# Second expert layer of a four-layer network: gate and up weights held still in one product, odd blocks stored from ScalarE's queue

## The reference

```python
logits = flat @ router_w.T
topk_scores, topk_idx = jax.lax.top_k(logits + router_bias, TOPK)      # TOPK = 2
topk_scores = jax.nn.softmax(topk_scores, axis=-1)
...
up_all = jnp.einsum('nd,kde->nke', flat, up_proj)       # (16, 128, 64)
gate_all = jnp.einsum('nd,kde->nke', flat, gate_proj)   # (16, 128, 64)
hidden = jax.nn.silu(gate_all) * up_all
down_all = jnp.einsum('nke,ked->nkd', hidden, down_proj)  # (16, 64, 128)
out = jnp.einsum('nk,nkd->nd', combine, down_all)
out = out + (jax.nn.silu(flat @ sh_gate.T) * (flat @ sh_up.T)) @ sh_down.T
```

## Time and profile before

| | us |
|---|---|
| Median of 3 runs | 928.29 |
| Lowest and highest run | 923.62, 928.73 |
| Span of the profiled execution, first to last instruction | 909.0 |
| The second layer's blocks, from the first gate-and-up product to the end of the last result copy | 484.60 to 536.16 |
| First TensorE instruction of the next attention | 538.38 |

### The profile page before, as it was taken

One profiled execution on the slowest core, in us unless ns is written; L12 is line 12 of the kernel. 1 busy time (PEld: TensorE's weight loads), 2 busy tenths in 40 slices (PEclk: granted clock), 3 DMA queues, 4 the chain that ended last, 5 costly groups with the idle time before them and its releaser, 6 DMA issues. The chain is left out here.

```text
span 909.0 us, 21425 instructions
## 1 busy us (share of the span) xinstructions
PE 777.9 (86%) x6462; PEld 591.8 (65%) x6462; DVE 599.4 (66%) x1816; ACT 504.2 (55%) x1391; POOL 414.8 (46%) x720
## 2 busy tenths in 40 slices
PE   3999996898679999999979977999969768669991
PEld 1566664798456778777747763666659546449991
DVE  5899995344567889888655447799947727633333
ACT  1577774676256776677635633677754422226663
POOL 3247766000534556765450018466217806824541
PEclk9999997999799999999989986799989775569996
DMA  8999941432000000100004431000000331122214
GB/s 254 384 401 404 289 195 35 90 90 57 23 7 14 14 15 24 26 22 11 19 25 100 114 85 28 16 23 23 2 1 2 98 102 41 46 54 64 74 51 153
DMA packets 69278, 78.96 MB, mean 87 GB/s; under 512 B 12848, under 2 KB 58560, under 8 KB 68912
## 3 DMA queue, kind: packets, MB, share of 16 engines
q1 hardware_dynamic: 59072, 62.15, 21.4%
q0 software_dynamic: 6368, 13.38, 5.1%
q10 hardware_dynamic: 3728, 2.07, 0.9%
HBM read 31.61 MB, written 45.96 MB: 85 GB/s over the span
## 5 line engine op out<-in xcount | busy, mean ns | idle before, releaser
L330 POOL DMA_INDIRECT routed_region<-routed_lines,line_slots x96 | 96.5, 1005 | 27.5 <-issue 23.6
L362 POOL DMA_INDIRECT late_results<-routed_region,line_slots x64 | 63.4, 990 | 77.4 <-remote 61.3
L774 ACT ACTIVATE probs_keymajor<-banks 128x512 f32<-128x512 f32 x128 | 70.2, 595 | 40.4 <-PE banks L584 40.4
L1401 PE MATMUL banks<-exps,work 128*128 128x128 f32 x624 | 85.5, 282 | 5.2 <-ACT exps L1475 5.0
L265 POOL TENSOR_TENSOR small<-small,half_and_eps 128x1 f32<-128x1 f32 x144 | 82.0, 569 | 11.3
L550 PE MATMUL banks<-work 32*128 32x512 f32 x256 | 80.9, 711 | 4.2 <-DVE exps L667 3.2
L658 DVE TENSOR_REDUCE small<-banks 128x8 f32<-128x1024 f32 x64 | 77.6, 1212 | 7.9 <-PE banks L550 3.9
L1401 PEld LDWEIGHTS banks<-exps,work 128*128 128x128 f32 x624 | 77.8, 196 | 7.5 <-ACT exps L1475 7.3
L667 DVE TENSOR_TENSOR exps<-banks,small 128x1024 f32<-128x1024 f32 x64 | 77.7, 1214 | 0.3
L584 PE MATMUL banks<-consts,exps 128*128 128x128 f32 x512 | 74.7, 294 | 1.1 <-ACT work L805 1.1
L584 PEld LDWEIGHTS banks<-consts,exps 128*128 128x128 f32 x512 | 61.1, 152 | 19.2 <-issue 13.0
(11 more groups left out here) (277 smaller groups left out, 1888.3 us busy)
## 6 DMA issues: line engine op xcount, KB each, us to landing
routed_region<-mid SPq DMA_DIRECT2D x52, 528.0 KB, 5.5
exps<-routed_region SPq DMA_DIRECT2D x125, 66.0 KB, 1.9
routed_region<-work SPq DMA_DIRECT2D x86, 64.0 KB, 1.8
weights_f<-in_weights_f SPq DMA_DIRECT2D x1, 4096.0 KB, 18.0
weights_f<-in_weights_f SPq DMA_DIRECT2D x3, 1024.0 KB, 10.9
shifted_rows<-work SPq DMA_DIRECT2D x16, 128.0 KB, 1.7
work<-expert_results SPq DMA_DIRECT2D x8, 256.0 KB, 5.0
routed_region<-routed_lines,line_slots POOLq DMA_INDIRECT x96, 2.4
```

Of the source, the lines that this page charges most:

```text
L330: nc.gpsimd.indirect_dma_start(k.regions[layer % 2], bass.IndirectOffsetOnAxis(k.slots[:, b, j:j + 1], 0), k.line[:, b % LINES, j, :], Non ...
L362: nc.gpsimd.indirect_dma_start(k.late[:, b % 2, j, :], None, k.regions[layer], bass.IndirectOffsetOnAxis(k.slots[:, b, j:j + 1], 0)).then_ ...
L774: nc.scalar.activation(k.pT[:, g * 512:(g + 1) * 512], bank[:, PT + g % 2, :], ACT.Copy).then_inc(s.pT, 1)
L1401: last = nc.tensor.matmul(bank[:, 2 + m % 4, i * T:(i + 1) * T], tile.weights[:, m % COPIES, i * 128:(i + 1) * 128], tile.gotT[:, m % 2, : ...
```

## The change

In the second layer the weights now take the way of the first layer, with GpSimd as the copier:

- GpSimd, after it has cleared the semaphores, copies each block's 128 columns of gate and up weights into the ring of four tiles (L1457 of the kernel before, now with `wide` = 128 columns).
- `up` waits for that copy, holds these weights still and streams the transposed tokens. Partitions 0 to 63 of the result are the up features, 64 to 127 the gate features (the two weight loads of the sublayer swap places), each 128 tokens long. The results use four banks of PSUM in place of two.
- ScalarE applies SiLU from partitions 64 to 127 into partitions 0 to 63, 128 elements each; VectorE multiplies into `tile.hid`, 64 partitions by 128, a ring of three. The lower half of `tile.hid` is zeroed once.
- The transpose of the inner values on TensorE and its copy on ScalarE are gone; `down` reads `tile.hid` directly.
- SyncE stores the even blocks only. ScalarE's queue stores the odd ones, four steps behind (`STORE_LAG`), inside ScalarE's loop; for that ScalarE reads the rows of the odd blocks into registers, four values at a time, every second entry of `rows_i`.

The diff, cut to its core:

```diff
-    t.hid = split(w[:, 0:2 * hidden], hidden)
+    t.hid = split(w[:, 0:3 * T], T)
...
-                for i, from_ in enumerate((E1 * H1, 0)):
+                for i, from_ in enumerate((0, E1 * H1)):
...
+    STORE_LAG = 4
+
+    def store(queue, m, row):
+        queue.wait_ge(s.y_out, m + 1)
+        queue.dma_start(region[bass.ds(row, T), 0:D], tile.y[:, m % RING, :]).then_inc(ld.stored[m % RING], 16)
...
-            if linear and m >= RING + 3:
-                store(m - RING - 3)
+            if linear and m >= RING + 3 and not (narrow and (m - RING - 3) % 2):
+                store(sp, m - RING - 3, rows_[m - RING - 3])
...
-            if m > 1:
-                pe.wait_ge(s.hid, m - 1)
-            nc.tensor.matmul(bank[:, 2 + m % 2, 0:wide], tile.gotT[:, m % 2, :], ups[:, bass.ds(offs[m], wide)],
-                             start=True, stop=True).then_inc(s.up, 1)
+            pe.wait_ge(s.copied, m + 1)
+            if m >= 4:
+                pe.wait_ge(s.hidT, m - 3)
+            for i in range(wide // T):
+                last = nc.tensor.matmul(bank[:, 2 + m % 4, i * T:(i + 1) * T],
+                                        tile.weights[:, m % COPIES, i * 128:(i + 1) * 128], tile.gotT[:, m % 2, :],
+                                        start=True, stop=True)
+            last.then_inc(s.up, 1)
...
-            if 0 <= t - 1 < nb and not by_feature:
-                hidden_T(t - 1)
...
-            copy(tile.weights[:, m % COPIES, :], ups[:, bass.ds(offs[m] * unit, 512)]).then_inc(s.copied, 1)
+            copy(tile.weights[:, m % COPIES, 0:wide], ups[:, bass.ds(offs[m] * unit, wide)]).then_inc(s.copied, 1)
...
+            if narrow:
+                nc.scalar.activation(tile.gate[0:H1, m % 2, 0:T], bank[H1:2 * H1, 2 + m % 4, 0:T],
+                                     ACT.Silu).then_inc(s.act, 1)
+                return
...
+        def store_odd(m):
+            if m // 2 == len(odd_rows):
+                odd_rows.extend(registers(mybir.EngineType.Activation, row_i[:, m:min(m + 8, nb):2],
+                                          REGIONS[layer % 2] * SHARE - T))
+            store(act, m, odd_rows[m // 2])
...
+        for t in range(-1, nb + (STORE_LAG if narrow else 2)):
...
-            if not by_feature and 0 <= t - 1 < nb:
-                hidden_T(t - 1)
+            if narrow and t >= STORE_LAG and (t - STORE_LAG) % 2:
+                store_odd(t - STORE_LAG)
...
+        if narrow:
+            v.memset(tile.hid[H1:128, :, :], 0.0).then_inc(s.padded, 1)
...
+            if narrow:
+                v.tensor_tensor(tile.hid[0:H1, m % hidden_ring, :], tile.gate[0:H1, m % 2, 0:T],
+                                bank[0:H1, 2 + m % 4, 0:T], ALU.mult).then_inc(s.hidT, 1)
                 return
...
+        if narrow:
+            copied = copy_weights(pool, mybir.EngineType.Pool, nc.gpsimd.tensor_copy, [], 1)
+            pool.wait_ge(s.steps, OFFS)
+            for m in range(nb):
+                copied(m)
```

More of the change, by code:

```diff
@@ L1223, in expert_layer @@
     biased = not gated
-    by_feature = hidden > H1
+    narrow = layer == 1
     tile = expert_tiles(k, max(hidden, 128), n, biased)
@@ L1230, in expert_layer @@
         s.act, = sems.new(tag, "act", True)
[L1231 to L1234, removed]
+    s.copied, = sems.new(tag, "copied", True)
     if shared:
@@ L1246, in expert_layer @@
     chunks = max(1, hidden // 128)
-    hidden_ring = 3 if by_feature else 2
+    hidden_ring = 3
     wide = 2 * hidden if gated else hidden
@@ L1395, in up, with down @@
             pe.wait_ge(s.xT_out, m + 1)
[L1396 to L1405, removed]
-            if m > 1:
-                pe.wait_ge(s.hid, m - 1)
-            nc.tensor.matmul(bank[:, 2 + m % 2, 0:wide], tile.gotT[:, m % 2, :], ups[:, bass.ds(offs[m], wide)],
-                             start=True, stop=True).then_inc(s.up, 1)
-        def hidden_T(m):
+            pe.wait_ge(s.copied, m + 1)
[6 more added lines that the diff above has]
+            last.then_inc(s.up, 1)
+        def down(m):
+            pe.wait_ge(s.hidT, m + 1)
             if shared and m == 0:
                 pe.wait_ge(s.sadd, 4)
[L1414 to L1423, removed]
+                pe.wait_ge(s.padded, 1)
             if m > 1:
                 pe.wait_ge(s.y_out, m - 1)
+            features = tile.hid if narrow else tile.hidT
             for i in range(chunks):
-                last = nc.tensor.matmul(bank[:, 6 + m % 2, 0:D], tile.hidT[:, m % hidden_ring, i * T:(i + 1) * T],
+                last = nc.tensor.matmul(bank[:, 6 + m % 2, 0:D], features[:, m % hidden_ring, i * T:(i + 1) * T],
                                         downs[:, bass.ds(offs[m] + (down_at + i * D), D)],
@@ L1481, in nonlinear @@
             if m > 1:
-                act.wait_ge(s.hidT if by_feature else s.hid, m - 1)
-            up_bank = bank[:, 2 + m % (4 if by_feature else 2), 0:hidden]
+                act.wait_ge(s.hidT, m - 1)
+            if narrow:
+                nc.scalar.activation(tile.gate[0:H1, m % 2, 0:T], bank[H1:2 * H1, 2 + m % 4, 0:T],
+                                     ACT.Silu).then_inc(s.act, 1)
+                return
+            up_bank = bank[:, 2 + m % 4, 0:hidden]
             nc.scalar.activation(tile.gate[:, m % 2, 0:hidden], up_bank, ACT.Silu).then_inc(s.act, 1)
         def hidden_T(m):
-            if shared and m == 0:
-                act.wait_ge(s.sy, 4)
-            act.wait_ge(s.up if by_feature else s.hT, m + 1)
+            act.wait_ge(s.up, m + 1)
             if m >= hidden_ring:
                 act.wait_ge(s.y, m - hidden_ring + 1)
-            if gated:
-                nc.scalar.activation(tile.hidT[:, m % 2, 0:chunks * T], bank[:, 4 + m % 2, 0:chunks * T],
-                                     ACT.Copy).then_inc(s.hidT, 1)
-                return
             if m % 8 == 0:
@@ L1512, in scalar @@
                 copied(m)
-        for t in range(-1, nb + 2):
+        odd_rows = []
+        def store_odd(m):
[4 more added lines that the diff above has]
+        if narrow:
+            act.wait_ge(s.steps, OFFS)
+        for t in range(-1, nb + (STORE_LAG if narrow else 2)):
             if 0 <= t + 1 < nb:
@@ L1519, in scalar @@
                 copied(t + COPIES - 1)
-            if by_feature and not gated and 0 <= t < nb:
+            if not gated and 0 <= t < nb:
                 hidden_T(t)
-            if not by_feature and 0 <= t - 1 < nb:
-                hidden_T(t - 1)
+            if narrow and t >= STORE_LAG and (t - STORE_LAG) % 2:
+                store_odd(t - STORE_LAG)
         if layer < 2:
@@ L1535, in vector @@
         v = nc.vector
-        if hidden < 128:
-            v.memset(tile.hid[:, :, hidden:128], 0.0).then_inc(s.padded, 1)
-            dve.wait_ge(s.padded, 1)
+        if narrow:
+            v.memset(tile.hid[H1:128, :, :], 0.0).then_inc(s.padded, 1)
         dve.wait_ge(s.sums, TOTALS)
```

20 lines of the change are left out of this document (6 added, 14 removed).

## The result

The changed kernel takes 917.29 us where the kernel before takes 923.36 (medians of 20 runs each on one chip). The ratio is 0.9923, 95% interval 0.9903 to 0.9944: 7.1 us less (5.2 to 9.0). It leaves out two slow executions of the changed kernel, 1430.71 and 2303.12 us, of which no trace was kept and whose cause is open, so it isn't the quotient of the two medians, which lie 6.1 us apart. The forecast was 7.6 us less. On another chip the pair came to 901.48 against 905.93, ratio 0.9943 (0.9911 to 0.9974), 5.2 us less (2.4 to 8.1).

A forecast was written before the change was run, and what follows sets the result against it. A latency loop early, SyncE's queue late. Start 486.5, steps 31.2, register loads 1.5 and 5.1, stretched stores 1.5, tail 1.8 make 527.6 against 536.16; less 0.95 at the end, 7.6 us gained: 920.7 us (8 in 10: 915.5 to 927.5).

The forecast's parts named there:

- What bounds the kernel: Second layer's blocks: early a latency loop of about 0.82 us a step, late SyncE's queue at 1.00 us a block.
- rival 4: Transfers bound and SyncE's queue only looked like the limit: 928 us; chance 0.25 together with rival 2 (gain eaten on ScalarE).
- TensorE: Without the transpose, instructions take 0.56 us a step, not 0.67; five register loads add 0.3 each, 1.5 us.
- ScalarE: Loop with a 0.61 us store gives 0.69 a step; six register loads add 5.1 us, stretched stores 1.5.
- First to last product: Steps 31.2 us, TensorE's register loads 1.5, ScalarE's register loads 5.1, stretched stores 1.5.
- a granted clock under 1.00: Sign of a wrong forecast: TensorE's longer pauses let its clock fall to the lower level; no size given.
- GpSimd: Copies of 0.28 us stay hidden; semaphore clearing delays the first product by 1.9 us, to 486.5 (bounds 1.4 and 2.5).
- The end: ScalarE's last odd store delays the exponential's table load, adding 0.95 us behind the last copy (bounds 0.3 and 1.2).
- SyncE after: Two loads and one store take 1.43 us, 0.72 a block; this queue alone would end the stage at 522.6.
- The first (SyncE's floor): Rival: shorter steps let SyncE's queue end the stage at 522.6, gain 12.6 us, 915.7 us; chance 0.16.
- The second: Rival: ScalarE's register loads of 1.77 us or steps of 0.81 leave 926.2 or 925.6; chance 0.25 shared with rival 4.
- The third: Rival: ScalarE's stores stretched by SyncE's issue, at 1.0 us each 932.9 us; chance 0.07 past 4.6 us slower.

The follow-up runs named there:

- e8_before_no_odd: Kernel before with the second layer's odd-block stores left out and nothing put on ScalarE: stage (second layer's blocks) 46.18 us, ratio 0.9891.
- e1_weights_only: Changed kernel with all stores on SyncE, keeping GpSimd's copies and the new product: stage 49.83 us, ratio 1.0000.
- e9_aligned_rows: Changed kernel with ScalarE reading eight neighbouring rows and using every second one: stage 45.35 us, ratio 0.9942.
- e3_early_copies: Changed kernel with GpSimd copying first and clearing two semaphores behind each copy: stage 43.06 us, ratio 0.9902.
- r_after_again: The changed kernel profiled and timed once more, unchanged, on another chip: stage 46.49 us, ratio 0.9943.
- e5_early_aligned: Changed kernel with GpSimd's copies ahead of the clearing and ScalarE reading eight neighbouring rows: stage 43.69 us, ratio 0.9912.
- e6_lagged: As e10_early_aligned_end, with SiLU and down product one step later, stores six steps behind, last odd stores (from block 40) on SyncE: stage 42.46 us, ratio 0.9901.
- e2_stores_only: Kernel before with only the odd stores moved to ScalarE, weights and transposes as before: stage 53.75 us, ratio 1.0029.
- e7_lagged_no_even: e6_lagged with the second layer's even-block stores left out, so SyncE only loads: stage 37.01 us, ratio 0.9866.
- e4_warm: Changed kernel with four unread 512-column products on TensorE ahead of its wait for GpSimd's first copy: stage 47.65 us.
- e10_early_aligned_end: e5_early_aligned with the last seven blocks' stores all on SyncE: stage 43.03 us, ratio 0.9888.

## Why the prediction was right, and where its sizes were off

The forecast was 920.7 us, 7.6 less, and the mechanism it names is the one that the runs show. Its last copy was due 527.6 - 483.88 = 43.7 us behind the `turn`; it came at 46.8, 3.1 later. By its own steps:

- **What bounds the kernel.** Right on both limits. Taking stores off SyncE alone makes the late slowdown go (e8_before_no_odd); making the loop faster alone runs into SyncE (e1_weights_only). "The late one is SyncE's queue" is shown, not only argued, and rival 4 (transfers bound) is out. The Trainium skill ("DMA: Bandwidth & Descriptors", Issuing engines are not separate DMA queues) has the sequencer's time as "usually small"; here half of the stores off that queue were worth 5.4 to 6.1 us of 52.
- **TensorE.** Step and register loads right: sets of six undisturbed steps between first products, as 0.66, 0.56, 0.77, 0.66, 0.78, 0.65, average 0.68 where 0.69 was forecast. TensorE's and ScalarE's register loads together lengthen eight steps by 1.72 + 1.11 - 2 × 0.68 = 1.5 us (forecast 0.9 + 0.3, and 0.3 for stretched stores).
- **ScalarE.** The store's instruction takes 0.34 where 0.42 was taken. The register load, the riskiest guess, was 0.89 to 0.97 with the last 0.68 (0.9 and 0.65), the six together 5.2 us (5.1); the reading that the price hangs on eight values in line is shown by e9_aligned_rows. Stretched stores: one in 23, 0.84 us (forecast one or two).
- **First to last product.** Forecast 31.2 + 1.5 + 5.1 + 1.5 = 39.3; at full clock it is 39.29 (e3_early_copies), in the changed kernel 40.82. Of the 1.5 us, 1.1 are a missing term: a pause of TensorE of 2.5 us and 3.4 us of half clock behind it; the other 0.4 are spread over later steps (0.1 in r_after_again). The prediction had named the sign, a granted clock under 1.00 behind TensorE's longer pauses, but gave it no price. It also took the clock before for 1.00 by its two stretches, while the kernel before has 3.4 us at half in the last eight of this stage: that loss went away with the late limit, inside the measured 536.16 from which the forecast starts, and without being named.
- **GpSimd.** Start late by 2.2 (1.9, bounds 1.4 to 2.5): the first register load took 0.79. Its copies were 293 ns (280 taken), hidden, and all 47 lie between 288 and 295, those beside VectorE's work too.
- **The tail behind the last product** was 545.39 to 548.46, 3.1 us, where 1.8 was taken. ScalarE's last register load (0.68, in my sum among the steps) and a store stand ahead of the last SiLU. So it costs at the tail, and not in a step. The steps took that much more, so that 39.3 and 39.29 agree partly by luck.
- **The end.** 0.6 later, 0.95 forecast; the table load starts with the last copy and doesn't come behind a whole store.
- **SyncE after.** The pitch of two loads and a store is 1.51 us, not 1.43: load to load is 0.52, and not the 0.43 of load to store, since a register operation of 37 ns stands ahead of a load and none ahead of a store. In the kernel before a store stood between any two loads late in the stage, and I took the load-to-store time for it. Harmless here, since this queue isn't the limit, but the floor of 522.6 was too early: in e5_early_aligned the last load was issued at 36.9 behind the `turn`, where 34.2 was forecast.
- **Rivals.** The first (SyncE's floor) isn't what happened, but it is what comes next: it stopped e5_early_aligned and e6_lagged. The second didn't occur, though its idea, gain eaten on ScalarE, is exactly e2_stores_only. The third, issue of a store stretched by SyncE's, is out: 22 of 23 stores took 0.34 to 0.41.

Sum of the misses on the last copy: 0.3 (start) + 1.5 (steps, 1.1 of it the clock) + 1.3 (tail) = 3.1. With 0.3 back at the end that makes 4.9 us of gain in the profile, and the second profiles show 4.5. The timings say 7.1 (5.2 to 9.0) and 5.2 (2.4 to 8.1). The second agrees with the profile; of the first some 2 us aren't in the stage, and where they are stays open: spans outside the stage differ by several us between profiles of kernels that are alike there. So the forecast of 7.6 lies as near as it does partly by that.

## What to carry to other kernels

Two limits that follow one another have to be lifted together: here neither half of the change alone made the kernel measurably faster (ratio 1.0000 and 1.0029; of the stage one gave 1.7 us and the other took 2.2), both together gave 0.9923 and 0.9943. Whoever moves work onto an engine that had none should look at what that engine does last before it: GpSimd's 65 semaphore clears cost 3.4 us, a third of them through TensorE's clock; copying first and clearing in between brought the kernel to 0.9902, and with aligned rows and the last stores left to SyncE to 0.9888 (0.9817 to 0.9959), which this study can't tell from 0.9901 of e6_lagged or 0.9902. The next limit is SyncE's queue again (e6_lagged against e7_lagged_no_even); what would lift it with all stores in place, such as fewer and larger transfers, wasn't tried.

## What the runs showed of the hardware that was not expected

- The price of a register load hangs on the form of the read: eight neighbouring values from a multiple of eight 0.53 to 0.64 us in the median of each engine (GpSimd's first 0.79), four of every second word 0.89 to 0.97, three 0.68, seven neighbours 0.94 to 1.3. The Trainium skill ("Runtime: NRT & Kernel Launch", Instruction fetch mechanics) has some 200 ns for each register "even for bulk"; four and three come near that, eight in line (0.07 each) don't. All of these are read from tables in SBUF; no run here shows the price from another memory.
- One pause of TensorE of 2.5 us, in a stretch that had been at full clock, is followed by 3.4 us at half; e1_weights_only and e9_aligned_rows, with such a pause, show the same, e3_early_copies and e4_warm, without it, don't. Falls late in the stage, again 3.4 us each, come in the kernel before, e1_weights_only, e2_stores_only, e4_warm, e6_lagged and e10_early_aligned_end. Mostly a stop of TensorE of around a us stands ahead, but that doesn't settle it: e4_warm fell behind one of 0.78 us, and r_after_again with 0.88 and 0.76 at the same place didn't.
- A load behind a load costs SyncE's queue 0.52 us, a store behind a load 0.43, a load behind a store 0.56, with instructions of 0.33 to 0.41. Single transfer instructions are stretched to 1.0 to 2.0 us. Before, they all fell beside a packet of instructions being fetched, and on ScalarE only one of 23 was hit in the changed kernel.
